# One mask operation for two neighbouring dense tiles, in a language-model tower on one core

## The reference, cut to what matters

```python
scores, idx = jax.lax.top_k(sim, PK_TOPK)
index = (idx0[..., :, None] + idx1[..., None, :]).reshape(b, n, HEADS, PK_TOPK * PK_TOPK)
score = (scores[0][..., :, None] + scores[1][..., None, :]).reshape(b, n, HEADS, PK_TOPK * PK_TOPK)
final_scores, pk_idx = jax.lax.top_k(score, FINAL_TOPK)
final_indices = jnp.take_along_axis(index, pk_idx, axis=-1)
final_scores = jax.nn.softmax(final_scores, axis=-1)
...
k = jnp.einsum('bnhk,bnhkd->bnhd', kv_scores, keys_table[ind])
v = jnp.einsum('bnhk,bnhkd->bnhd', kv_scores, values_table[ind])
```

## Time and profile before

| | us |
|---|---|
| median of 3 runs | 3269.15 |
| lowest, highest | 3267.7, 3270.88 |
| span of the profiled execution | 3918.3 |
| PE, DVE, ACT, POOL busy in it | 3008.9, 2785.8, 2039.4, 2057.7 |
| mean granted clock of PE in it | 0.862 |

### The profile page before, as it was taken

One profiled execution on the slowest core, in us unless ns is written; L12 is line 12 of the kernel. 1 busy time (PEld: TensorE's weight loads), 2 busy tenths in 40 slices (PEclk: granted clock), 3 DMA queues, 4 the chain that ended last, 5 costly groups with the idle time before them and its releaser, 6 DMA issues.

```text
span 3918.3 us, 39268 instructions
## 1 busy us (share of the span) xinstructions
PE 3008.9 (77%) x9722; PEld 1391.1 (36%) x9722; DVE 2785.8 (71%) x9999; ACT 2039.4 (52%) x4498; POOL 2057.7 (53%) x2095
## 2 busy tenths in 40 slices
PE   4861657878787878878778868888778878888888
PEld 2430223333333333333333433333333433333343
DVE  7678777777777777776777887777768786874433
ACT  3231545555555555655555655556555655555532
POOL 3011666666656665555565655556656655655400
PEclk8985777888787888989888989888888988989899
DMA  1001121212121111112121212111111212121100
GB/s 37 22 8 52 44 66 43 62 45 57 48 56 47 52 52 50 52 46 55 44 59 38 65 40 57 44 52 53 51 50 46 57 46 56 42 62 39 33 3 3
DMA packets 85626, 179.86 MB, mean 46 GB/s; under 512 B 40177, under 2 KB 41107, under 8 KB 85398
## 3 DMA queue, kind: packets, MB, share of 16 engines
q0 software_dynamic: 66560, 135.40, 13.1%
q1 hardware_dynamic: 18838, 41.94, 3.5%
HBM read 176.15 MB, written 1.05 MB: 45 GB/s over the span
## 4 chain that ended last, share of the span: by engine, by line
PE 41%; DVE 25%; another core or an unknown queue 11%; issue 8%; ACT 8%; ACTq 0%; DVEq 0%
PE mx_acc L1430 12%; PE mx_O L1442 7%; PE mx_area L1476 6%; DVE mx_W L1787 5%; PE mx_D L1420 4%; ACT mx_GT L1691 3%; DVE mx_KVs L2013 3%; PE mx_area L1456 2%; ACT mx_W L1623 2%; DVE mx_mx_part L2031 2%; PE mx_area L1492 1%; DVE mx_mx L2031 1%; PE mx_X L1560 1%; PE mx_area L1486 1%
## 5 line engine op out<-in xcount | busy, mean ns | idle before, releaser
L1402 POOL DMA_INDIRECT mx_G<-in_kv_table,mx_slot_i x2048 | 2004.0, 978 | 1394.6 <-issue 590.1
L1430 PE MATMUL mx_acc<-mx_W,mx_table 128*128 128x512 f32 x2048 | 1180.7, 660 | 1.6 <-ACT mx_kvT L1630 0.7
L1787 DVE SCALAR_TENSOR_TENSOR mx_W<-mx_D,mx_W 128x512 f32<-128x512 f32 x1024 | 699.1, 683 | 297.5 <-ACT mx_W L1623 180.5
L1623 ACT ACTIVATE mx_W<-mx_D 128x512 f32<-128x512 f32 x1024 | 606.6, 593 | 523.2 <-PE mx_D L1420 231.0
L1691 ACT ACTIVATE mx_GT<-mx_G,mx_slot_w 128x128 f32<-128x128 f32 x2048 | 759.2, 495 | 3.2 <-DVE mx_KVs L2013 1.1
L1420 PE MATMUL mx_D<-mx_U,mx_pick_b 96*128 96x512 bf16 x1024 | 432.7, 423 | 110.8 <-DVE mx_W L1787 52.5
L1430 PEld LDWEIGHTS mx_acc<-mx_W,mx_table 128*128 128x128 f32 x2048 | 436.1, 214 | 201.9 <-issue 104.5
L1647 ACT ACTIVATE mx_PT<-mx_area 128x512 f32<-128x512 f32 x472 | 241.8, 514 | 464.9 <-PE mx_area L1480 146.3
L1442 PE MATMUL mx_O<-mx_PT,mx_KVs 128*65 128x512 f32 (+3 forms) x768 | 347.5, 536 | 170.0 <-ACT mx_PT L1647 82.8
L1456 PE MATMUL mx_area<-mx_KTa,mx_QTa 64*128 64x512 f32 (+3 forms) x384 | 200.6, 607 | 132.6 <-DVE mx_mx L2031 66.1
L2013 DVE TENSOR_REDUCE mx_KVs<-mx_GT 128x128 f32<-128x2048 f32 x128 | 291.9, 2280 | 6.0 <-ACT mx_GT L1691 5.9
(11 more groups left out here) (390 smaller groups left out, 4462.4 us busy)
## 6 DMA issues: line engine op xcount, KB each, us to landing
mx_table<-in_kv_dense SPq DMA_DIRECT2D x64, 512.0 KB
mx_G<-in_kv_table,mx_slot_i POOLq DMA_INDIRECT x2048
tz_table<-in_c_dft SPq DMA_DIRECT2D x1, 2048.0 KB
tz_table<-in_c_idft SPq DMA_DIRECT2D x8, 256.0 KB, 2.6
out_h<-mx_xc SPq DMA_DIRECT2D x4, 256.0 KB
mx_G<-in_c_pick SPq DMA_DIRECT2D x1, 528.0 KB
st_h<-in_tok_W,em_ids POOLq DMA_INDIRECT x32
st_keys<-in_pk_keys SPq DMA_DIRECT2D x1, 512.0 KB, 3.9
```

The lines of the kernel that those rows point to most:

```text
L1402: pool.indirect_dma_start(G[g % RING][:, r, :], None, a["kv_table"], bass.IndirectOffsetOnAxis(slot_i[n % 2][:, k, r:r + 1], 0))\
L1430: pe.matmul(acc[:, :], table[:, tile, :], W[c % TILE_RING][:, :], start=(tile == 0), stop=(tile == TILES - 1)).then_inc(applied, 1)
L1623: act.activation(W[c % TILE_RING][:, :], D_ps[c % 3][:, :], ACT.Exp).then_inc(p_done, 1)
L1787: dve.scalar_tensor_tensor(W[c % TILE_RING][:, :], D_ps[c % 3][:, :], 0.0, W[c % TILE_RING][:, :], ALU.is_ge, ALU.mult).then_inc(w_done, 1)
```

## The change

DVE masks two tiles, c - 1 and c with c odd, in one operation of 128 x 1024, at the even positions; the odd positions have no mask. For that the three D banks are one tensor of neighbouring banks, and the tiles take them in the order 0, 1, 2, 1 (`BANK_OF`), so that a pair is always banks 0 and 1 or banks 1 and 2. Every odd tile takes bank 1. In the ring of W the two tiles of every second pair stand in reverse (`W_of`), as their banks do. The score of an odd tile k now waits for the pair (k - 3, k - 2), before for mask k - 3; that of an even tile waits for the pair (k - 4, k - 3). The table's rows are laid out in another order, done on the host before the launch, and 4 of 32 tiles are fresh instead of 6. POOL's gathers are released in fours, for each two tiles masked: the third and fourth of a four go with the first two.

```diff
+BANK_OF = (0, 1, 2, 1)
...
 def corner_of(tile):
-    bank, step = tile % 3, tile // 3
-    pair, eighth = (bank, step) if step < 8 else (3, 3 * bank + step - 8)
-    return pair // 2, pair % 2, eighth, step in (0, 8)
+    if tile % 2:
+        pair, eighth = 2 + tile // 16, tile // 2 % 8
+    else:
+        pair, eighth = tile // 2 % 2, tile // 4
+    return pair // 2, pair % 2, eighth, eighth == 0
...
-        W = [m.sb(f"W{i}", [P, HALF]) for i in range(TILE_RING)]
+        W_ring = m.sb("W", [P, TILE_RING, HALF])
...
-        D_ps = [m.ps(f"D{i}", [P, HALF]) for i in range(3)]
+        D_banks = m.ps("D", [P, 3, HALF])
+        D_ps = [D_banks[:, i, :] for i in range(3)]
...
+        def D_of(c):
+            return D_banks[:, BANK_OF[c % 4], :]
+
+        def W_of(c):
+            first = c // 2 * 2 % TILE_RING
+            return W_ring[:, first + (c + c // 2) % 2, :]
+
+        def pair_of_banks(c):
+            lower = c // 2 % 2
+            return D_banks[:, lower:lower + 2, :]
+
+        def pair_of_W(c):
+            first = c // 2 * 2 % TILE_RING
+            return W_ring[:, first:first + 2, :]
...
-                    ahead = SLOT * n + 8 * k - 6 + r // 2
-                    if r % 2 == 0 and ahead > 0:
+                    ahead = SLOT * n + 8 * k - 6 + r // 4 * 2
+                    if r % 4 == 0 and ahead > 0:
                         pool.wait_ge(w_done, ahead)
...
-                if c >= 3:
-                    pe.wait_ge(w_done, c - 2)
+                if c >= 4:
+                    pe.wait_ge(w_done, c - 1 if c % 2 else c - 2)
+                elif c == 3:
+                    pe.wait_ge(w_done, 2)
...
-                step = 1 + eighth // 3 if fresh else 3 + eighth
+                step = 1 if fresh else 3 + eighth
...
             def exp_dense(c):
                 act.wait_ge(d_ready, c + 1)
                 if c >= TILE_RING:
-                    act.wait_ge(applied, c - TILE_RING + 1)
-                act.activation(W[c % TILE_RING][:, :], D_ps[c % 3][:, :], ACT.Exp).then_inc(p_done, 1)
+                    act.wait_ge(applied, c // 2 * 2 - TILE_RING + 2)
+                act.activation(W_of(c), D_of(c), ACT.Exp).then_inc(p_done, 1)
...
-            def mask_dense(c):
+            def mask_pair(c):
                 dve.wait_ge(p_done, c + 1)
-                dve.scalar_tensor_tensor(W[c % TILE_RING][:, :], D_ps[c % 3][:, :], 0.0, W[c % TILE_RING][:, :],
-                                         ALU.is_ge, ALU.mult).then_inc(w_done, 1)
+                dve.scalar_tensor_tensor(pair_of_W(c), pair_of_banks(c), 0.0, pair_of_W(c),
+                                         ALU.is_ge, ALU.mult).then_inc(w_done, 2)
...
                 def mask_of_position():
-                    if 0 <= c + 3 < PAIRS * SLOT and not masked:
-                        mask_dense(c + 3)
+                    if 0 <= c + 3 < PAIRS * SLOT and c % 2 == 0 and not masked:
+                        mask_pair(c + 3)
```

More of the change, by code:

```diff
@@ L1413, in score_dense @@
                     pe.wait_ge(x_taken, cnt.x["U", n, 2 * half + 1] + 1)
-                if c >= 3:
-                    pe.wait_ge(w_done, c - 2)
+                if c >= 4:
+                    pe.wait_ge(w_done, c - 1 if c % 2 else c - 2)
+                elif c == 3:
+                    pe.wait_ge(w_done, 2)
                 if fresh:
-                    pe.matmul(D_ps[c % 3][:, :], pick_b[:, 0, :], U[n % 2][:, 2 + jh, cols], start=True, stop=False,
+                    pe.matmul(D_of(c), pick_b[:, 0, :], U[n % 2][:, 2 + jh, cols], start=True, stop=False,
                               skip_group_check=True)
-                step = 1 + eighth // 3 if fresh else 3 + eighth
-                pe.matmul(D_ps[c % 3][:, :], pick_b[:, step, :], U[n % 2][:, ih, cols],
+                step = 1 if fresh else 3 + eighth
+                pe.matmul(D_of(c), pick_b[:, step, :], U[n % 2][:, ih, cols],
                           start=False, stop=True, skip_group_check=True).then_inc(d_ready, 1)
@@ L1429, in apply_dense @@
                 pe.wait_ge(w_done, c + 1)
-                pe.matmul(acc[:, :], table[:, tile, :], W[c % TILE_RING][:, :], start=(tile == 0),
+                pe.matmul(acc[:, :], table[:, tile, :], W_of(c), start=(tile == 0),
                           stop=(tile == TILES - 1)).then_inc(applied, 1)
```

## The result

| | median, us | lowest, highest | ratio to before, 95% interval |
|---|---|---|---|
| before, 4 runs beside the changed kernel | 3268.43 | 3266.13, 3270.88 | 1 |
| changed, 4 runs | 3289.89 | 3288.5, 3291.01 | 1.0057 [1.0043, 1.007] |

The changed kernel is slower by 21.5 us, 0.66% by the medians and 0.57% by the ratio (19 us, 14 to 23 by the interval). The forecast was 3283 us, slower by 14 us. The ratios leave out executions at a much lower granted clock, of which there was one here: 4183.87 us at 0.642, in the last experiment.

A forecast was written before the change was run, and what follows sets the result against it. No engine alone bounds the kernel: stretches go through DVE or PE alone, PE holding 41% of the chain, DVE 25%. DVE -2, PE -7 and wait +26 make +17 us, scaled +14: 3283 us, range 3232 to 3325 us.

The forecast's parts named there:

- The pair and its neighbours: On DVE, 512 double masks save 36 us from start to start; uncovered waits give back 30 us: net 6 us.
- Rival 4: DVE's pair gets no cheaper than two masks (1.37 us): +29 us in all, 3293 us, chance 0.03.
- The two factors: A microsecond taken from an engine is worth chain share over busy share: 0.35 for DVE, 0.53 for PE.
- The new wait: PE's odd-tile score waits for a pair: 49 us, the middle of 35 and 63 without cover, costing 26 us.
- Positions 16 to 41: PE's next score products there wait for the previous position's maxima anyway, so added waits there were not counted.
- Waits on DVE: DVE stood 180 us for exps before masks; the change in this was put at nothing, at best 31 us gained.
- Gathers: POOL's earlier gathers set at 0; they could bring at most the 3.2 us ACT stood before weighing gathered rows.
- The scale of 0.834: The sum over the profiled span of 3918.3 us was scaled to the shorter timed runs: +17 us became +14.
- Rival 1: Faster: DVE bounds more of the timed runs, 74 us by records count, PE's wait is absorbed: 3241 us, chance 0.33.
- Rival 2: No change: PE's wait costs 18 us, DVE saves 13 us and PE 7 us: 3268 us, chance 0.22.
- Rival 3: Slower: at every eighth position DVE sums gathered rows right before the pair, PE's idle covers nothing: 3324 us, chance 0.12.
- what would show it: Signs: pair record near 1.22 us, 64 fewer fresh matmuls, PE's 111 us of waits before scores growing by some 100 us.

The follow-up runs named there:

- the last experiment: The kernel before with 12 of 32 tiles fresh in place of 6, 192 matmuls more for PE: 3277.85 us, 1.0015.
- order alone: Against the kernel before: new bank order, table layout with four fresh tiles and gathers in fours, but one mask per tile at each position: 3275.46 us, 1.0024.
- two masks at one position: The changed kernel with the pair's operation split into two masks of 512 columns, both at the even position: 3295.76 us, 1.0084.

## Why the prediction held, point by point

**The pair and its neighbours: right.** 1.13 us from start to start and 0.64 for dependent operations, as forecast. DVE's busy time falls by 2748.4 - 2735.7 = 12.7 us. The forecast of 6 counts from start to start, and so takes in the idle gaps of under 0.06 us between operations, which grow by 8 us (668 to 904 of them): 4 or 5 us saved, as forecast. Both terms were a little too large: the pairs save 30 us, not 36, and the lost places cost 17 + 8 = 25 us, not 30 (the gaps grow by 244 from order alone to two masks at one position, and the prediction counted 256 places). Rival 4 is refuted by the pair's record.

**The two factors: wrong, by half or more.** 0.35 for DVE is 0.15 by the shorter masks (0.18 at a like clock), 0.53 for PE is 0.12 by the fresh tiles (0.26). The failed step is "a microsecond taken from an engine is worth its share of the chain over its busy share". PE and DVE are each busy for 84 or 85% and POOL issues almost without a break, so that what is taken from one is soon waited for from the next: 47 of DVE's 79 us came back as waits for exps. By the measured factors the two gains are 1 us and 2 to 4 us, and not 2 + 7.

**The new wait: the right mechanism, and about the right size by two errors.** The forecast was 49 us of PE at 0.53, 26 us, 22 when scaled. The runs give 19 to 21.5 us in all plus 3 to 5 us of gains: some 25 us, about 10 of it with the order alone. That the forecast of 14 us came near the result is thus luck: the count was too large, its price too small. But the 49 us was counted in the execution of 3918.3 us. In the one profiled again the score of the odd tile began before mask k - 2 ended in 134 of 511 cases, by 162 us, not 158 and 298 us; outside positions 16 to 41 it is 51 cases and 40 us, 32 without cover, and with the 0.53 us added 102 cases and 78 us with the cap, 69 without cover. The middle of 32 and 69, at PE's measured factor, would give 6 us (13 at a like clock). So the waits cost more than their microseconds times PE's factor. Why is not shown. My reading is that the score heads a chain through ACT and DVE to the next pair, so that a long delay goes round to the engine that caused it; no run isolated this, and the matmuls added to the fresh tiles, which stand in front of scores too, speak for it only if a delay of 0.22 us still finds cover there and one of a microsecond or more doesn't.

**Positions 16 to 41: half right.** For the order alone the new waits there were given back, as the prediction held. For the pair they were not: tiles 20, 34, 36, 38 and 44 lose 0.2 to 0.5 us in each slot.

**Waits on DVE set at nothing: right.** 208.6 us for exps before, 208.2 after.

**Gathers set at nothing: right as a sum, wrong as reasoning.** The fours alone changed nothing. But "POOL's 547 us are slack" and "ACT stood 3.2 us" are rows of the longer execution; in the one profiled again POOL is 9% of the chain and then 12%. And the fours were part of the price: without them the pairs cost 21 us more, since POOL waits for pairs that come by twos. The prediction named the last four of a block as no later, which holds for fours only.

**The scale of 0.834: unfounded.** It shrank all terms alike, while the excess of 649 us of span was not spread alike: PE, at a granted clock of 0.862, was busy for 223 us more, DVE for 37, ACT for 22, POOL for 1, and each engine waited for the rest. It made 17 into 14, on the wrong side.

**The rivals.** Rival 1 (faster, 0.33) falls with DVE's factor: even its 74 us are 11 at 0.15. Rival 2 (no change) set 20 us of gains for DVE and PE, which are 3 to 5, against a wait of 18, which is some 25. Rival 3 asked where the burst of sum and pair decides: the piece at 1838 us shows it at work, but the time is 3290, not 3324, and taking the burst apart made it worse. In "what would show it", the growth of PE's waits came (+136 us at the weight loads of the line of scores, 120 with those of the fresh tiles; forecast 100), and was no proof: the order alone shows the same growth at less than half of the cost.

No version beat the kernel before: 0.9991 and 0.9996, with the gathers earlier and in fours, hold 1 in their intervals. The runs that are faster, with 12 gathers or with masks of 438 columns, leave out a part of the work.

## What to carry to other kernels

Merging two small operations saves a fixed part of one (0.06 to 0.07 us here) and delays the first result until the second is done; in a ring of three buffers whoever waits for a buffer loses a step of lead for it. Here the new order and the joint position cost 28 us, and the merging gave back 9 (0 to 18). Before a profile is used for factors, its span is to be set beside the timed runs: one that is 20% longer shows the durations of DVE, ACT and POOL rightly (a mask 682 and 680 ns) and those of PE (an application 660 and 620 ns), the waits, the slack and the chain not. Where several engines are each busy for more than 80%, what one of them is worth should be taken from a run that adds or removes plain work on it, with the granted clock of the runs beside their times, not from its share of the chain.

## What the runs showed of the hardware that was not expected

- Indirect gathers issued by POOL start 1.25 us apart, though each one's record is 0.94 us. Leaving out 4 of 16 took 87 us from a kernel of 3267.
- Among runs of one and the same kernel the granted clock goes from 0.921 to 0.929, and 0.01 of it goes with 10 to 12 us of 3270. The work of two kernels can't be compared to a few us without it.
- A DVE operation can start about 0.08 us before its forerunner's record ends (1700.64 + 1.22 against 1701.77), but not one that waits for it by a semaphore: the hot rows are 0.64 us apart with records of 0.61. The Trainium skill ("VectorE: DVE Perf Modes", section "The DRAIN you can't avoid") says that the semaphore costs nothing extra; here a wait for the forerunner's semaphore costs about 0.11 us (0.63 against 0.52 us from start to start), and 17 us of busy time and 8 us of gaps over the kernel where pairing uncovered it.
